# A recurrent gate with a selector layer on eight cores: element-wise work of the scan moved between the gate groups, squares of the layer norm moved to GpSimd

## The reference

```python
x = layernorm(input)                             # over 1024 channels
gate, xa = split(x @ w_in.T)                     # first product, 2048 columns
xc = causal_conv4(xa) + b_conv
forget, inp = split(xc @ w_gates.T + b_gates)    # second product, 2048 columns
alpha = exp(-8 * softplus(forget_base) * sigmoid(forget))
u = sqrt(1 - alpha**2 + 1e-6) * sigmoid(inp) * xc
h = scan over time of h = alpha * h + u
s = (gelu(gate) * h) @ w_out.T                   # last product, 1024 columns
logits = x @ sel_w.T                             # 8192 columns, 8 per output channel
comp = x @ comp_w.T                              # 8192 columns, 8 per output channel
out = input + s * silu(comp of the largest logit per channel)
```

## Time and profile before

| | us |
|---|---|
| median of 4 executions | 4040.6 |
| the four executions | 3952.61, 4463.78, 3957.41, 4123.79 |
| the profiled execution | 3952.17 |
| its span, slowest core (core 3) | 3950.2 |
| spans of the eight cores | 3933.5 to 3950.2 |
| busy: TensorE matmul, VectorE, GpSimd, ScalarE | 3612.8, 1565.7, 1515.0, 1141.2 |

### The profile page before, as it was taken

How to read it: one execution, slowest core, us unless ns; L and a number is a source line. 1 busy time by engine, 2 the same in 40 slices (tenths; PEclk the granted TensorE clock), 3 DMA queues, 4 the chain that set the end, 5 groups by cost and what they waited for, 6 DMA issues and landing times.

```text
span 3950.2 us, 46754 instructions; the slowest of 8 cores (3933.5 to 3950.2 us)
## 1 busy us (share of the span) xinstructions
PE 3612.8 (91%) x16272; PEld 1602.1 (41%) x16272; DVE 1565.7 (40%) x1696; ACT 1141.2 (29%) x1331; POOL 1515.0 (38%) x752
## 2 busy tenths in 40 slices
PE   2997999999689899999968989999996999999997
PEld 0443444444234344444323434444432444444443
DVE  2414433342541543334263253334426245344433
ACT  1333222223133332222323432222222343222221
POOL 1333444443234344444323344444422344444442
PEclk8998999999799899999989999999997999999999
DMA  2232333332322233333232223333323223333332
GB/s 76 86 102 91 104 100 107 97 107 86 94 88 94 89 107 107 97 107 96 86 96 96 93 91 104 104 100 105 98 75 107 96 86 96 105 98 98 106 107 75
DMA packets 366871, 380.61 MB, mean 96 GB/s; under 512 B 12304, under 2 KB 356384, under 8 KB 366640
## 3 DMA queue, kind: packets, MB, share of 16 engines
q1 hardware_dynamic: 364032, 369.15, 29.3%
q0 software_dynamic: 2608, 8.49, 0.7%
HBM read 369.20 MB, written 8.39 MB: 96 GB/s over the span
## 4 chain that ended last, share of the span: by engine, by line
PE 76%; DVE 11%; DMA 3%; POOL 3%; ACT 3%; issue 2%; DVEq 0%; SPq 0%; POOLq 0%; ACTq 0%
PE pg L273 75%; DVE poolC L86 3%; POOL wl L86 3%; DMA poolA<-xT 3%; DVE poolB L86 2%; DVE xnl L86 1%; DVE hb L86 1%; PE pg L340 1%; PE pg L334 1%; DVE mxb L86 1%; ACT wh L86 1%; DVE msk L86 1%; DVE accb L86 1%; ACT sf L86 1%; DVE scr L86 1%
## 5 line engine op out<-in xcount | busy, mean ns | idle before, releaser
L86 POOL TENSOR_TENSOR wl<-w,wh 128x1024 bf16<-128x1024 f32 x672 | 1473.8, 2193 | 2208.7 <-ACT wh L86 2158.5
L273 PE MATMUL pg<-xnh,wh 128*128 128x512 bf16 x4608 | 1765.7, 383 | 220.1 <-POOL wl L86 196.6
L273 PE MATMUL pg<-xnl,wh 128*128 128x512 bf16 x4608 | 1764.6, 383 | 0.0
L273 PE MATMUL pg<-xnh,wl 128*128 128x512 bf16 x4608 | 1763.1, 383 | 0.0
L86 ACT ACTIVATE wh<-w 128x1024 bf16<-128x1024 f32 x672 | 710.1, 1057 | 1650.6 <-PE pg L273 1612.1
L273 PEld LDWEIGHTS pg<-xnh,wh 128*128 128x128 bf16 x4608 | 454.3, 99 | 786.0 <-issue 254.5
L86 DVE TENSOR_SCALAR si<-pg,vecsb 128x512 f32<-128x512 f32 x256 | 192.2, 751 | 1387.6 <-PE pg L273 1386.2
L273 PEld LDWEIGHTS pg<-xnh,wl 128*128 128x128 bf16 x4608 | 454.8, 99 | 556.4 <-issue 22.1
L273 PEld LDWEIGHTS pg<-xnl,wh 128*128 128x128 bf16 x4608 | 454.2, 99 | 550.9 <-issue 18.6
L273 PE MATMUL pg<-xch,wh 128*128 128x512 bf16 x768 | 295.1, 384 | 45.3 <-POOL wl L86 45.3
L86 DVE SCALAR_TENSOR_TENSOR msk<-sf,vecsb,mxb 128x512 uint8<-128x512 f32 x256 | 285.7, 1116 | 27.4 <-DVE msk L86 0.9
(11 more groups left out here) (56 smaller groups left out, 817.5 us busy)
## 6 DMA issues: line engine op xcount, KB each, us to landing
w<-selT SPq DMA_DIRECT2D x256, 512.0 KB, 4.7
w<-cmpT SPq DMA_DIRECT2D x256, 512.0 KB, 4.8
w<-w1T SPq DMA_DIRECT2D x64, 512.0 KB, 4.9
w<-w2T SPq DMA_DIRECT2D x64, 512.0 KB, 4.4
w<-w3T SPq DMA_DIRECT2D x32, 512.0 KB, 4.8
hb<-xT POOLq DMA_DIRECT2D x32, 256.0 KB, 3.4
poolA<-xT SPq DMA_DIRECT2D x32, 256.0 KB, 3.6
outT<-poolC SPq DMA_DIRECT2D x32, 256.0 KB, 2.3
```

Source lines behind the costliest of these rows:

```text
L86: return fn(*a, **k)
L273: last = tensor.matmul(bank[:, :], wop[:, wcol:wcol + P], xop[:, k * TT:(k + 1) * TT], start=(idx == 0), stop=(idx == 23))
```

## The change

Two edits. First, the element-wise work of a chunk is cut in two. `emit_EL_a` holds everything up to the scan and the carry, `emit_EL_b` holds y, its split and the load of the next x. The second product's groups run in the order 0, 1, 8, 9, 2, 3, 10, 11 and so on, so that after each fourth group both `sf` and `si` of two chunks are there, and `emit_EL_a` of these two follows at once. `emit_EL_b` stays behind the selector groups of block 0. The list of weight halves follows the new order. Second, the squares of the layer norm are made by GpSimd (a product of `hb` with itself) and no longer by ScalarE.

```diff
-    for s in range(4):
-        half_list.append((w2T, s * TT))
-        half_list.append((w2T, s * TT + HW))
+    for p2 in range(4):
+        half_list.append((w2T, p2 * HW))
+        half_list.append((w2T, 1024 + p2 * HW))
...
-                    c.needt(scalar, "sc", xtok)
-                    c.needt(scalar, "sc", free_A[sl])
-                    ins = scalar.activation(
+                    c.needt(gpsimd, "gp", xtok)
+                    c.needt(gpsimd, "gp", free_A[sl])
+                    ins = gpsimd.tensor_tensor(
                         poolA[:, sl * TT:(sl + 1) * TT],
-                        hb[:, k * TT:(k + 1) * TT], AF.Square)
-                    sq_rdy = ("sc", c.inc(ins, "sc"))
+                        hb[:, k * TT:(k + 1) * TT],
+                        hb[:, k * TT:(k + 1) * TT], OP.mult)
+                    sq_rdy = ("gpc", c.inc(ins, "gpc"))
...
-                def emit_EL_chunk(k):
+                def emit_EL_a(k):
...
+
+                def emit_EL_b(k):
+                    sl = k % 2
+                    HBk = hb[:, k * TT:(k + 1) * TT]
                     c.needt(vector, "ve", free_B[sl])
                     PB = poolB[:, sl * TT:(sl + 1) * TT]
...
+                g2_order = []
+                for p2 in range(4):
+                    g2_order += [2 * p2, 2 * p2 + 1, 8 + 2 * p2, 9 + 2 * p2]
+                for j2, m in enumerate(g2_order):
+                    par = (t * NH + 8 + j2 // 2) % 2
+                    bidx = next_bank()
+                    gtok = mm_group(bidx, par, (j2 % 2) * P, xch, xcl,
+                                    extra=[xc_rdy])
...
+                    if j2 % 4 == 3:
+                        p2 = j2 // 4
+                        emit_EL_a(2 * p2)
+                        emit_EL_a(2 * p2 + 1)
+
...
                         if i == 0:
-                            emit_EL_chunk(n)
+                            emit_EL_b(n)
```

More of the change, by code:

```diff
@@ L479, in _ @@
                         free_C[sl] = xc_rdy
[L480 to L502, removed]
                 c.needt(scalar, "sc", ce_tok)
@@ L572, in emit_EL_chunk @@
                         emit_xload(t + 1, k)
+                g2_order = []
[6 more added lines that the diff above has]
+                                    extra=[xc_rdy])
+                    if j2 % 2 == 1:
+                        whl_free[par] = gtok
+                        load_next_half()
+                    if j2 == 15:
+                        free_xc_pe[0] = gtok
+                    c.needt(scalar, "sc", gtok)
+                    if m < 8:
+                        c.need(scalar, "sc", "ve", free_sf[m][1]) if free_sf[m] else None
+                        ins = scalar.activation(
+                            sf[:, m * TT:(m + 1) * TT], pg[bidx][:, :],
+                            AF.Sigmoid, bias=vecs[:, C_BGF + m:C_BGF + m + 1])
+                    else:
+                        c.needt(scalar, "sc", free_si[0])
+                        ins = scalar.activation(
+                            si[:, (m - 8) * TT:(m - 7) * TT], pg[bidx][:, :],
+                            AF.Sigmoid,
+                            bias=vecs[:, C_BGI + (m - 8):C_BGI + (m - 8) + 1])
+                    bank_free[bidx] = ("sc", c.inc(ins, "sc"))
+                    if j2 % 4 == 3:
+                        p2 = j2 // 4
+                        emit_EL_a(2 * p2)
+                        emit_EL_a(2 * p2 + 1)
                 silu_toks = [None] * KC
```

## The result

The changed kernel runs in 0.9779 of the time before, 95% interval 0.9764 to 0.9794: 2.2% faster. Seven executions lie between 3863.5 and 3870.7 us; the profiled one took 3865.8, with a span of 3863.9 on its slowest core. The forecast was 3877 us and, by a narrow margin, a change within 2%. The range, 3848 to 3945 us, covered nearly all that the move could give or fail to give, so lying in it says little.

What follows compares the result with a forecast made beforehand. The prediction took TensorE's waits for late weight splits to bound the kernel. Span 3950.2 us, less 90.3 (120.5 - 13.7 - 16.5), plus 15.3 for squares, plus 2.0 outside the span, gave 3877 us; range 3848 to 3945.

Steps and rivals of the forecast that it cites:

- Where the time was lost, and that the move recovers it: Tiles 0 to 3, from selector product on: late weight splits lose TensorE 120.5 us, the most the move can give.
- 13 stalls of 1.05 us: Second product, behind chunk pairs, 3 places in tiles 0 to 2, 4 in tile 3: late split stops TensorE, 13.7 us.
- The stop at the selector product: Last pair, tiles 0 to 2: x load waiting for y delays the split; 3.8 plus 1.7 us clock, total 16.5.
- The two engines take turns: Chunk work: POOL and two-input VectorE operations exclude each other, so the second scr ends late; stall 1.05 us, without it 0.
- rival without meetings: Chunk work: scr finds its port free, the 13 stalls vanish, the last three are 2.7 us; 3851 to 3855, chance 0.24.
- Squares, 15.3 us lost: Norm ahead of tiles 1 to 3: POOL's squares stand behind the subtraction pair, 5.1 us each time, 15.3 in all.
- Table loads without a gap: ScalarE: each table load costs 1.28 us only; the rival adds a 1.4 us gap, 3939 us, chance 0.02.
- The clock at small stops: Second product: TensorE keeps its full clock behind the 13 small stops, so they cost no clock loss.
- rival at 3899: Second product: clock falls at the 13 small stops too, 1.7 us each, 22 more; chance 0.15 together with longer stalls.
- The side of the 2%: Whole kernel: forecast 4 us short of 2% faster (3873 us); chances 0.46 faster, 0.50 within, 0.04 slower.

Runs made afterwards that it cites:

- longer pair: Changed kernel with one more in-place ScalarE copy of 512 columns behind each pair of chunks; ratio 0.978, 3864.1 to 3867.4 us.
- shortened first pair: Changed kernel with GpSimd's step 1 - scr left out for chunks 0 and 1 of each tile, ScalarE's Ln doing it; profiled execution 3868.1 us.

## Why the prediction was right or wrong

**Where the time was lost, and that the move recovers it: right.** 120.5 us of loss were read from the chain, 18.3 are left.

**13 stalls of 1.05 us: wrong, and this is the step that failed.** The step treated each place by itself, with the due time at 20.4 behind the pair's `wh` copy. A stop delays the matmuls but not the start of the next pair, so the next split has that much more time. Measured in core 0 are eight stops, two a tile, of 0.36 to 0.74 us idle, in place of 13. The term stood in the sum with 13.7 us and measured 5.4 (4.1 idle, and 0.16 more at each stop): 8.3 of the 12 us by which the move gained more than forecast. Of these, 5 stops fewer make 5.3 us, and the smaller size the rest. The chain's length was nearly right, 20.9 to 21.0 us against 21.3, but a due time so near turned that difference into a third of the stall: 0.73 in place of 1.05 behind pair 0. The fourth place of tile 3 should not have been counted for another reason: the sum put a table load there, and it is not needed. The experiments with the longer pair and the shortened first pair show the carrying over, one by growing stops at the same places, the other by moving them.

**The stop at the selector product, 3.8 us and 1.7 of clock, three times: mechanism right, size too large.** It stood in the sum with 16.5 us and measured 12.9, the rest of the 18.3. The split ended at 285.75 (281.07 + 4.68), 23.9 us after the pair's `wh` copy at 261.82; the forecast had 24.0. But here too the stop before had moved the due time, and TensorE was idle for 2.89 us. The clock fell behind it in core 0 in all three tiles, but not in every core (last section). The x load behind the split removed the stop.

```profile
280.46 0.59 POOL L86 DMA_DIRECT2D hb<-xT  x1 [7.39 <-DVE xch L86]
281.07 4.68 POOL L86 TENSOR_TENSOR wl<-w,wh 128x1024 bf16<-128x1024 f32 x2
```

The first x load of tile 0 waits for y 7.39 us, as the x loads did before (7.11 to 7.48), but once a tile and not eight times. The next two waited 0.56 and 1.33 us, where the forecast had them find y ready; no stop came of it.

**The two engines take turns: right.** POOL's second `scr` took 1.09 us in place of 0.62. The Trainium skill, page "SBUF — State Buffer", section "SBUF: two separate sides", states that one of the two engines holds the port pair they share for a whole instruction, and this trace agrees with it. The rival without meetings would have given 3851 to 3855; the measured time lies between it and the forecast, but not for its reason.

**Squares, 15.3 us lost: right.** Alone they cost 16.6 us (8 to 25 by the interval), which is the price of their place behind the subtractions; a square took 1.04 to 1.11 us against 1.1, the wait 6.29 against 6.3.

**Table loads without a gap: right.** 232.57 and 1.28 long; the Sigmoid behind it began at 233.86, 0.01 us later.

**The clock at small stops: right that they keep it.** In core 0 the 2 us behind each of the eight stops have a granted 1.00. The rival at 3899 did not come.

**The side of the 2%.** The forecast was 75 us gained, 4 us short of 2%, with 0.46 for more and 0.50 for less. It was 86 to 87. The two terms of stalls, 12 us too large together, less 1 us for the squares, make about this difference. A sum so near a bound deserved the question whether its small repeated terms were independent of each other; they were taken as 13 and 3 equal copies.

## What to carry to other kernels

When an engine that works ahead of TensorE is started by TensorE's progress, a stop of TensorE is slack for the next round: repeated small overruns do not simply add up (here eight stops stood where 13 were counted), so follow the due times through two rounds before you multiply. Work for the next stage whose inputs are long there (here the squares) belongs ahead of refilling a buffer that is due later, and the choice of engine mattered less than this place. A DMA issue that waits for data holds what is queued behind it; put it behind the work that is due first.

## What the runs showed of the hardware

TensorE's clock fell behind some stops at the selector product and not behind others of the same length. In tile 1 of the changed kernel all eight cores were idle there for 2.86 or 2.87 us. Windows of TensorE right behind this stop, in cores 0, 1 and 7, each at its own time (us, busy, granted clock, DMA share, GB/s):

```profile
core 0: us, PE busy (x), PEclk, DMA share, GB/s
1247.60:1252.00 4.40, 4.32 (x13) 0.61 0.54 135
...
core 1: us, PE busy (x), PEclk, DMA share, GB/s
1238.10:1242.50 4.40, 4.36 (x21) 1.00 0.76 243
...
core 7: us, PE busy (x), PEclk, DMA share, GB/s
1243.60:1248.00 4.40, 4.40 (x13) 0.61 0.66 151
```

Cores 0 and 7 were granted 0.61, a mix of 1.2 and 2.4 GHz, and made 13 matmuls where core 1, at 2.4 GHz, made 21. Core 4 fell too (0.69), and cores 2, 3, 5 and 6 kept 1.00. In tile 2, where the stop was shorter, 2.49 to 2.52 us, seven of the eight cores fell and core 4 kept 1.00. Such a fall cost 1.4 to 1.7 us: in core 0 the 2976 matmuls behind it took 643.86 and 644.18 us where their number is worth 642.5.

Over tiles 0 to 2 and all cores, the clock fell behind 16 of the 24 stops of the changed kernel (2.49 to 3.11 us), behind 1 of 24 with the longer pair (1.86 to 2.38 us, the fall at 2.00) and behind 19 of 24 with the shortened first pair (3.33 to 3.73 us). So the clock was kept more often behind the shorter stops, and the kernel with the added copy, whose last stop is shorter, had almost none of these falls. But the length alone does not decide; what else does, these runs do not show.
